# First attention in double periods: the scores of four units, then two weighted sums

## The reference

```
qkv = u @ W_qkv                                  # u: [32, 128, 128], W_qkv: [128, 3072]
q, k, v = split(qkv, 3)                          # 16 heads of 64
score = einsum('bihd,bjhd->bijh', q, k) / 8
wmat = softmax(score * mask + 1e30 * (mask - 1), axis=2)      # mask: lower triangle
out = einsum('bijh,bjhd->bihd', wmat, v).reshape(b, 128, 1024)
x1 = x + out @ W_out
```

## Time and profile before

| | |
|---|---|
| median of 3 runs | 1017.48 us (1017.44 to 1018.26) |
| span of the profiled execution | 1016.5 us |
| TensorE busy | 977.0 us (96%), granted clock 1.00 in the stretches of the first attention |
| VectorE busy | 876.8 us (86%) |
| ScalarE busy | 831.3 us (82%) |
| GpSimd busy | 471.2 us (46%) |
| first attention | about 12 to 435 us of the span |

### The profile page before, as it was taken

How to read it: one execution, slowest core, us unless ns; L and a number is a source line. 1 busy time by engine, 2 the same in 40 slices (tenths; PEclk the granted TensorE clock), 3 DMA queues, 4 the chain that set the end, 5 groups by cost and what they waited for, 6 DMA issues and landing times.

```text
span 1016.5 us, 25956 instructions
## 1 busy us (share of the span) xinstructions
PE 977.0 (96%) x8939; PEld 789.2 (78%) x8939; DVE 876.8 (86%) x3718; ACT 831.3 (82%) x2232; POOL 471.2 (46%) x541
## 2 busy tenths in 40 slices
PE   7999999999999999999989999999999999999897
PEld 6898888888888989743268988888777777776566
DVE  6777989898989888799998899889988888896985
ACT  6888888888888888887797878776887888886786
POOL 2334545454545463606810112102887888893041
PEclk9999999999999999999999999999999999999999
DMA  9000000000000000000000000000000000000002
GB/s 376 35 2 2 2 2 2 2 2 2 2 2 2 2 2 2 2 1 0 1 1 1 1 1 1 1 11 11 23 23 23 23 23 23 23 3 1 1 2 84
DMA packets 8723, 18.31 MB, mean 18 GB/s; under 512 B 1296, under 2 KB 5648, under 8 KB 8208
## 3 DMA queue, kind: packets, MB, share of 16 engines
q1 hardware_dynamic: 8592, 16.65, 4.9%
HBM read 10.36 MB, written 2.10 MB: 12 GB/s over the span
## 4 chain that ended last, share of the span: by engine, by line
PE 79%; DVE 9%; ACT 6%; POOL 3%; issue 3%; DMA 0%; DVEq 0%; ACTq 0%; POOLq 0%
PE PB L245 8%; PE PB L246 8%; PE PB L247 8%; PE PB L341 6%; PE PB L396 6%; PE PB L379 6%; PE PB L1798 5%; PE PB L1195 3%; PE PB L1770 3%; PE PB L1197 3%; PE PB L1196 3%; PE PB L1815 3%; PE PB L428 2%; PE PB L429 1%; PE PB L430 1%
## 5 line engine op out<-in xcount | busy, mean ns | idle before, releaser
L371 POOL TENSOR_TENSOR W<-W,small 128x512 f32<-128x512 f32 x128 | 138.5, 1082 | 216.3 <-DVE small L365 216.3
L360 ACT ACTIVATE W<-W,small 128x128 f32<-128x128 f32 x512 | 198.8, 390 | 29.6 <-DVE small L351 29.0
L245 PE MATMUL PB<-RR_s 128*128 128x256 f32 (+3 forms) x568 | 184.4, 325 | 3.5 <-issue 1.9
L246 PE MATMUL PB<-RR_s 128*128 128x256 f32 (+3 forms) x568 | 176.8, 311 | 0.0
L247 PE MATMUL PB<-RR_s 128*128 128x256 f32 (+3 forms) x568 | 176.7, 311 | 0.0
L351 DVE CUSTOM_DVE_ANT_0 W<-PB,W 128x128 f32<-128x128 f32 x512 | 117.3, 284 | 39.1 <-PE PB L341 38.1
L1786 POOL TENSOR_TENSOR AR_s<-AR_s,small 128x512 f32<-128x512 f32 x128 | 129.3, 1040 | 15.9 <-DVE small L1779 15.8
L1169 ACT ACTIVATE AR_s<-PB,W 128x512 f32<-128x512 f32 (+2 forms) x160 | 100.5, 629 | 28.5 <-PE PB L247 22.1
L245 PEld LDWEIGHTS PB<-RR_s 128*128 128x128 f32 x568 | 108.6, 191 | 11.1 <-issue 4.2
L1183 DVE TENSOR_TENSOR RR_s<-AR_s,RR_s 128x512 fp32r<-128x512 f32 (+2 forms) x160 | 100.4, 636 | 17.1 <-ACT RR_s L1174 13.8
L1779 DVE CUSTOM_DVE_ANT_0 AR_s<-PB,W 128x128 f32<-128x128 f32 x512 | 111.0, 286 | 2.6 <-PE PB L1770 0.9
(11 more groups left out here) (385 smaller groups left out, 2437.0 us busy)
## 6 DMA issues: line engine op xcount, KB each, us to landing
W<-in_w SPq DMA_DIRECT2D x1, 5809.5 KB, 25.5
W<-in_w SPq DMA_DIRECT2D x2, 1024.0 KB, 7.2
out<-XT SPq DMA_DIRECT2D x8, 256.0 KB, 2.3
XF<-in_xT SPq DMA_DIRECT2D x3, 512.0 KB, 10.9
W<-AR_s SPq DMA_DIRECT2D x16, 64.0 KB, 2.1
AR_s<-AR_s SPq DMA_DIRECT2D x16, 64.0 KB, 2.1
QS<-AR_s SPq DMA_DIRECT2D x12, 64.0 KB, 2.1
KR<-AR_s SPq DMA_DIRECT2D x12, 64.0 KB, 2.1
```

The costliest lines, as they stand in the source:

```text
L245: nc.tensor.matmul(out, lh, rh, start=True, stop=False)
L246: nc.tensor.matmul(out, ll, rh, start=False, stop=False)
L360: e = nc.scalar.activation(SS[r][:, hl], SS[r][:, hl], ACTF.Exp, bias=mx[r][:, h:h + 1], scale=-1.0, accum_out=rc[r][:, h:h + 1])
L371: nc.gpsimd.tensor_tensor(s3, s3, over(rc[r], 2, [128, 4, 128]), ALU.mult).then_inc(s_nrm, 1)
```

## The change

Two periods become one **double period** z (NP = 32). TensorE issues the scores of four units in a row, then two weighted sums in a row (of periods 2z-4 and 2z-3), and the four transposes stand singly between projections. Scores use the banks in pairs of units: units 4z and 4z+1 share PB0 and PB1, units 4z+2 and 4z+3 share PB2 and PB3, and a maximum waits for both units of its pair. Tiles for scores, maxima and sums grow from 6 to 8, the query/key tiles shrink from three pairs to two. The exponentials of every fourth unit, and of the second, are cut in two halves of two heads. The list of `passes` follows the new order.

```
-        QK = [[ar(512) for _ in range(2)] for _ in range(3)]
+        QK = [[ar(512) for _ in range(2)] for _ in range(2)]
-        SS = [cs(w(x), i) for x in ("wq", "wk", "wv") for i in range(2)]
+        SS = [cs(w(x), i) for x in ("wq", "wk", "wv") for i in range(2)] + [ar(512) for _ in range(2)]
...
+        for z in range(NP):
+            if z + 1 < NP:
+                passes("k", 4 * z + 4, s_qk, 4 * z + 5)
+                passes("k", 4 * z + 5, s_qk, 4 * z + 6)
+            passes("v", 2 * z, s_vp, 2 * z + 1)
+            plan_gates(2 * z)
+            if z % 2 == 0 and z // 2 + 1 < NCH:
+                passes("u", z // 2 + 1, s_uf, z // 2 + 2)
+            if z >= 2:
+                passes("y", z - 2, s_y, z - 1)
+            if z + 1 < NP:
+                passes("k", 4 * z + 6, s_qk, 4 * z + 7)
+                passes("k", 4 * z + 7, s_qk, 4 * z + 8)
+            passes("v", 2 * z + 1, s_vp, 2 * z + 2)
+            plan_gates(2 * z + 1)
+            if z:
+                passes("o", 2 * z - 2, s_ot, 2 * z - 1)
+                passes("o", 2 * z - 1, s_ot, 2 * z)
...
         def dve_qk(n):
             v, pr = divmod(n, 2)
-            dve.wait_ge(s_S, 2 * (v - 3) + 2)
+            dve.wait_ge(s_S, 2 * (v - 2) + 2)
...
         def score(u, h):
-            return PB[2 * (u % 2) + h % 2][:, h // 2 * 128:h // 2 * 128 + 128]
+            at = u % 2 * 256 + h // 2 * 128
+            return PB[2 * (u // 2 % 2) + h % 2][:, at:at + 128]
...
         def pe_S(u):
-            pe.wait_ge(s_max, 4 * (u - 1))
+            pe.wait_ge(s_max, 8 * (u // 2 - 1))
...
         def dve_max(u):
-            dve.wait_ge(s_T, u - 5)
-            dve.wait_ge(s_S, u + 1)
+            dve.wait_ge(s_T, u - 7)
+            dve.wait_ge(s_S, 2 * (u // 2) + 2)
```

TensorE's new list, then VectorE's:

```
+            for z in range(NP - 1):
+                for u in range(4 * z, 4 * z + 4):
+                    pe_S(u)
+                if z >= 2:
+                    pe_PV(2 * z - 4)
+                    pe_PV(2 * z - 3)
+                pe_k(4 * z + 4)
+                if z:
+                    pe_T(4 * z - 4)
+                pe_k(4 * z + 5)
+                if z:
+                    pe_T(4 * z - 3)
+                pe_v(2 * z)
+                pe_gates(2 * z)
+                if z % 2 == 0 and z // 2 + 1 < NCH:
+                    pe_u(z // 2 + 1)
+                if z:
+                    pe_T(4 * z - 2)
+                if z >= 2:
+                    pe_y(z - 2)
+                pe_k(4 * z + 6)
+                if z:
+                    pe_T(4 * z - 1)
+                pe_k(4 * z + 7)
+                pe_v(2 * z + 1)
+                pe_gates(2 * z + 1)
...
+            for z in range(NP):
+                dve_max(4 * z)
+                if z:
+                    dve_rc(4 * z - 1)
+                for c in range(1, 4):
+                    dve_max(4 * z + c)
+                dve_rc(4 * z)
+                if z >= 2:
+                    dve_ot(2 * z - 4)
+                    dve_ot(2 * z - 3)
+                for n in (4 * z + 4, 4 * z + 5):
+                    if z + 1 < NP:
+                        dve_qk(n)
+                dve_rc(4 * z + 1)
+                if z % 2 == 0 and z // 2 + 1 < NCH:
+                    dve_uf(z // 2 + 1)
+                dve_gates(4 * z)
+                dve_gates(4 * z + 1)
+                if z >= 2:
+                    dve_y(z - 2)
+                if z + 1 < NP:
+                    dve_qk(4 * z + 6)
+                if z % 2 == 0 and z // 2 + 1 < NCH:
+                    dve_ul(z // 2 + 1)
+                for s in split_steps(2 * z + 1):
+                    dve_xl(*s)
+                dve_rc(4 * z + 2)
+                if z + 1 < NP:
+                    dve_qk(4 * z + 7)
+                dve_gates(4 * z + 2)
+                dve_gates(4 * z + 3)
```

ScalarE's new list (the weights of later steps left out):

```
+            for z in range(NP):
+                if z:
+                    act_exp(4 * z - 1, (2, 3))
+                act_exp(4 * z)
+                act_exp(4 * z + 1, (0, 1))
+                if z >= 2:
+                    act_oh(2 * z - 4)
+                    act_oh(2 * z - 3)
+                if z:
+                    act_pt(4 * z - 4)
+                act_exp(4 * z + 1, (2, 3))
+                if z:
+                    act_pt(4 * z - 3)
+                act_vp(2 * z)
+                act_gates(2 * z)
+                if z:
+                    act_pt(4 * z - 2)
+                act_exp(4 * z + 2)
...
+                if z:
+                    act_pt(4 * z - 1)
+                if z + 1 < NP:
+                    act_exp(4 * z + 3, (0, 1))
+                    act_vp(2 * z + 1)
+                    act_gates(2 * z + 1)
```

## The result

The changed kernel takes 1023.74 us (median, 1022.76 to 1025.53), the kernel before 1017.46 (1016.48 to 1018.26) beside it. The ratio is 1.0059, interval 1.0045 to 1.0073: 6.3 us slower, by over 0.2%. The profiled spans say the same, 1023.1 against 1016.5.

The account below looks back on a forecast made before the run. TensorE bounds, with a new wait on VectorE's read of a shared bank: +4.3 for chunks with gates, +0.2 before them, -2.2 fill and drain, +2.3 on 1016.5; the median stands 1.0 above, so 1019.8, range 1009 to 1027.

Parts of the forecast that it names:

- rival 3: VectorE stays late: maxima start about 0.4 late in every double period with gates; 1024.3, to 1027; chance 0.15.
- The wait on k(4z+5): TensorE's second key projection waits for VectorE's lower half to read a shared bank: 5.52 against 5.08, 0.44 per double period.
- VectorE's lateness: After u and gate h, late gate reciprocals delay the next maxima: 0.9 us per chunk, bounds 0.3 and 1.5.
- The u matmul: A u matmul on TensorE adds some 0.77 us to its period, before as after the change.
- Changes of shape: TensorE going to another matmul shape costs 0.15 to 0.16; six changes per two periods become three.
- The transposes' bank: One bank holds all transposes: 1.27 needed between two, 1.15 available, so 0.12 lost at the third transpose.
- Fill and tail: Scores of period 4's place reached at about 31.9 instead of 36.84, 2.7 owed in the tail: gain 2.2, bounds 0 and 4.
- (1): The saved changes arrive whole, lower half read before 5.08: chunk 50.6, time 1004; chance 0.15.
- (2): The bank wait stays but the gate steps fit, no lateness: chunk 52.00, time 1013.9; chance 0.25.

Follow-up runs that it names:

- experiment 1: Changed kernel with VectorE's first query/key copy of a double period ahead of the two lower halves of weighted sums: 1047.91 us, ratio 1.0296 to the kernel before.
- experiment 2: Changed kernel with VectorE's first lower half ahead of the last four maxima, ScalarE's upper halves moved to match: 1013.26 us, ratio 0.9964 to the kernel before.
- experiment 3: Changed kernel with gate steps 4 and 5 (two reciprocals) moved into the middle of the next double period: 1019.89 us, ratio 1.0025 to the kernel before.
- Experiment 7: Kernel of experiment 6 with ScalarE's first upper half moved between the two halves of the first exponential: 1016.27 us, ratio 0.9994 to the kernel before.
- experiment 5: Kernel of experiment 4 with the transposes moved further apart, ScalarE's copies following: 1018.68 us, ratio 1.0013 to the kernel before.
- experiment 8: Kernel of experiment 5 with both lower halves ahead of the last four maxima and both upper halves earlier: 1010.23 us, ratio 0.9934 to the kernel before.
- experiment 4: Changed kernel with the edits of experiment 2 and experiment 3 together: 1008.72 us, ratio 0.9912 to the kernel before.
- experiment 6: Kernel of experiment 4 with the two weighted sums pulled apart, each behind two units of scores, first lower half moved to match: 1033.67 us, ratio 1.0163.

## Why the prediction came out as it did

The forecast was 1019.8, the time 1023.7: inside the range, slower as the chances leaned, just inside the forecast's own part of it (1016 to 1024) and 0.6 below the bottom of rival 3 (1024.3). The mechanism of the forecast is what happened; experiments 1 and 2 show it in both directions. Several of its terms were mis-sized, some of them in opposite directions, so that the time came out as near as it did partly by luck.

**The wait on k(4z+5): right.** The loop was put at first maximum plus 4.29. Measured from the first maximum to k(4z+5): 4.34, 4.19, 4.25, 4.22. Due 5.08 was 5.06. So the wait is "first maximum + 4.25 - 5.06", and all that was off is when the first maximum starts.

| double period | forecast | measured | first maximum, forecast | measured | wait, forecast | measured |
|---|---|---|---|---|---|---|
| u | 12.80 | 12.53 | 1.23 | 1.32 | 0.44 | 0.51 |
| two gates | 13.55 | 13.95 | 1.23 | 1.62 | 0.44 | 0.78 |
| u, one gate | 13.50 | 13.31 | 1.23 | 1.32 | 0.44 | 0.60 |
| plain, after gates | 13.05 | 13.47 | 2.1 | 2.57 | 1.34 | 1.70 |
| chunk | 52.90 | 53.26 | | | 2.66 | 3.59 |

**VectorE's lateness: the term that was too small.** "I take 0.9" for one double period a chunk was too little, inside its bound of 1.5. In that one it was 1.25 (2.57 less 1.32): the first maximum came 15.88 after the chunk's start where the reciprocals were forecast to end at 15.6, and the scores that it is measured against came at 13.31, not 13.50. Of the 0.28, 0.15 is that GpSimd's additions started at 11.45 instead of 11.3; the rest is mostly the additions themselves, 2.75 up to the start of the reciprocals where two times 1.29 were counted. And a second double period (two gates) was 0.3 late, which the forecast left at nothing and rival 3 held. Experiment 3 takes the first lateness alone away and gets 1.17 of that double period back.

**The u matmul: too dear.** Forecast 0.77 from the earlier trace rows, measured 0.44 (253.78 to 254.22). The 6.06 of the old period held a wait besides the matmul: there the u matmul started at 256.59, three matmuls of 0.12 behind one at 255.97, so 0.26 late, and the transpose came 0.50 behind it. That is 0.66 per chunk on the other side, so the two errors nearly cancel: waits +0.93, u -0.66, and 0.1 of rest are the chunk's +0.36. This is the luck: with the u matmul at its measured price the forecast would have been some 4.6 us lower (14 of them in the 29 double periods), about 1015.

**Changes of shape: right.** 0.15 to 0.16 each was read from gaps. Experiment 7 measures 0.35 for two, so 0.17 to 0.18 each. The rows gave a fair price for an operation that no row shows alone.

**The transposes' bank: right as a term, but nothing to be gained there.** 0.12 was forecast at the third transpose, 0.13 is there (267.51 due, 267.64 started). The forecast leaves open what removing it would buy; in the two orders tried, experiments 5 and 8, it was nothing, because another wait took its place.

**Fill and tail: half right.** The scores of z = 2 start at 33.73, where those of period 4 started at 36.77 in TensorE's timeline: gain 3.0, forecast 4.9. (In experiments 1 and 2, whose lists are the same up to there, these scores start at 34.03 and 32.08, so the 3.0 is good to about a microsecond.) The walk had no waits, and there are two, 1.09 for a copy of keys and 1.02 for a copy of transposes, as the rows of the fill show:

```profile
21.02 0.67 PE L283 MATMUL PB<-HF,W 128*128 128x256 f32 x2 [1.09 <-DVE AR_s L323]
...
29.02 0.66 PE L394 MATMUL PB<-W 128*128 128x128 f32 x4 [1.02 <-ACT XT L400]
```

The tail is 3.7 longer (31.29 against 27.57), forecast 2.7. The total: -3.0 fill, +6.85 over 29 double periods (384.67 against 377.82), +3.7 tail, -0.9 behind the recurrence (where the kernel before has the stretch of low clock and the changed one has not), is +6.6. The forecast had -4.9, +4.5, +2.7. Why TensorE in the tail waits for copies and lower halves, 1.8 us in three places of the changed kernel, was not tried, nor whether another order shortens it; nor was the fill.

**The rivals.** (1), the changes arrive whole: not in this order, but experiment 4 has it with the same TensorE list, so "maxima faster" was not needed, only the lower half ahead of four of them and the gate reciprocals later. (2), no lateness: not so; experiment 3 shows what it would be, chunk 52.1 where 52.00 was reckoned. (3), VectorE late throughout: in part, 0.3 in the double period of two gates, nothing in the other two; the time comes next to its lower end by that and by the smaller gain of the fill. By VectorE's busy sum (47.13 of 53.26) nothing binds; the row of 18.5 us of waits decides against the sum. The Trainium skill, page "TensorEngine Tiling (Array Packing)", section "PSUM Bottleneck", says that packing does not speed up the emptying of PSUM, which may become the limit. This trace agrees in that the emptying of one bank did set the pace, but by its place in VectorE's order and not by VectorE's total work. The same section advises sharing the emptying between ScalarE and VectorE; here that is done, and experiment 6 shows its price where one waits for the other (23.0 us of VectorE's time).

## What to carry to other kernels

When matmuls are grouped to save time on TensorE, list what rotates through the same PSUM banks and walk to the reader that must be done three places on; its position in its engine's list, not that engine's busy share, sets the period. If the group makes the reader late, move that one reader ahead of work of the same engine that nobody waits for (10.5 us between the changed kernel and experiment 2), and move what it waits for on the other engine too (17.4 us between experiments 6 and 7). A wait that another instruction covers comes back as soon as that instruction is moved. And before a difference of a few microseconds is put down to an order, look at the granted clock of both profiles: here 4.0 us of experiment 1, and 1.6 us between the two kinds of profile, were the clock's.

## What the runs showed that I had not expected

- An order on ScalarE alone, one copy of 0.58 us moved past two exponentials of 0.39, is worth 17.4 us in the median and 16.0 in the stage (experiments 6 and 7).
- The first maximum starts 1.32 behind the scores, and waits for 16 passes; the earlier trace rows has the next block 1.09 behind 16 passes. So some 0.23 lies between the end of issue and VectorE's start; in the earlier trace rows, with eight passes, the whole was 0.77.
- A matmul stream that shows no idle time can still wait: in experiment 4 TensorE is busy for 50.84 of 50.88 us, and yet its starts give away waits of 0.33 in the transposes of the plain double period and 0.2 in a block of scores.
- The granted clock fell to its lower level behind three of five waits of 2.04 or 2.05 us in experiment 1, and not behind the other two.
